# Attention and a top-1 expert layer on one core: the product of the last group of tokens put ahead of the work of the group before it, and the routing of the last four groups put later

## The chip, the cores and the metric

One core of one Trainium2 chip. The metric is the time of one execution on the device in microseconds (us); lower is better.

## What the reference computes

`x` is 64 x 64 tokens of 128 numbers, `ctx` is 64 x 64 tokens of 64 numbers; all data are float32.

```python
def xattn(query, key, value):            # 64 sequences, 64 queries, 64 keys each
    q, k, v = query @ Wq + bq, key @ Wk + bk, value @ Wv + bv
    return softmax(q @ k.T) @ v
def ffn(h):                              # h: 4096 tokens x 128; 8 experts, 512 hidden
    route = sigmoid(h @ Wr + br)
    e = argmax(route, axis=1)            # one expert for each token
    return max(route) * (gelu(h @ W1[e]) @ W2[e])
x = x + tanh(g_xattn) * xattn(layernorm(x), ctx, ctx)
x = x + tanh(g_ffn) * ffn(layernorm(x))
```

## The kernel before

Each engine has an instruction list that is written out by hand, and the engines meet at semaphores. SP issues plain loads, GpSimd (POOL) issues DMAs whose rows go to computed addresses, TensorE (PE) multiplies, ScalarE (ACT) does exp, tanh, gelu and copies, VectorE (DVE) does the rest. An engine that waits blocks everything behind it in its own list.

**Attention part.** The 4096 tokens are 32 tiles of 128, in 8 groups `g` of 4 tiles. Loop `k` runs over the groups on PE, ACT and DVE. In PE's list `scores(k)` forms the products of queries and keys, DVE takes `row_maxima(k)`, ACT takes `exp_scores(k)`, PE does `transpose_probs(k)`, ACT copies it (`copy_probsT`), and PE does `attend(k)`, the product with the values (L1398, 16 matmuls), whose last matmul increments `attn_done`. `project(k + 1)` makes the next queries once DVE's `route_x(k)` has read their bank. DVE's block of `k + 1` begins with `sums(k)`, which waits for `attn_done`, and adds `residual(k, t)`.

**Routing.** `scale_logits(g)`, `bias_logits(g)`, ACT's `tanh_logits(g)` and DVE's `choose(g, 0..6)` choose each token's expert. PE's `prefix(g)` counts the tokens ahead of it, and `place_of_group(g)` and `place_rows(g)` (L762) give the row of the DRAM tensor `scratch` that the token goes to. Each expert has a region there.

**POOL.** In the loop over `at` (L504) POOL writes one tile of 128 token rows a time to `scratch` (L484, 32 times). Before the first tile of a group it waits until that group is placed. `RSTD2_AT` says behind which of the 32 writes the variance of which later group is raised to -1/2 (`rstd2`, L480, a computation and not a DMA). `scatter_tile(j)` (L499) writes finished expert tiles to the output: 4 of them ahead of the writes of group 7 (`EARLY_RESULTS`), the other 32 behind all of them.

**Expert part.** The experts' rows are cut into 25 full tiles `j` of 128 rows and 11 pairs of half tiles. They are laid out in stages as more groups have been placed: `STAGES` holds for each stage how many groups must have been counted and up to which tile it goes. DVE's chain `copy_counts` ... `place_tiles` ... `take_tiles` writes the table of a stage, and SP loads its tiles (L361) when the table is there and the rows of its groups have been written. For each tile ACT normalises the rows (`normalise_tile`, L603) and copies its expert's first weights (L542), PE transposes it (`transpose_tile`, L1445), DVE copies that to SBUF (`copy_transposed`, L1038), PE multiplies (`up`, L1489), ACT takes gelu (L611), PE multiplies (`down`, L1501) and DVE adds (`residual2`, L1043). In PE's loop over `j` the order is `down(j)`, `transpose_tile(j + 3)`, `up(j + 2)`. DVE's loop over `j` is `residual2(j)`, `copy_transposed(j + 3)`, and then the pieces of routing and tables put at this `j`.

Waits are written as `wait_ge(semaphore, count)`; `after(engine, semaphore, g)` waits until step `g` has been done.

Of the kernel before, what the change touches and what calls it, by code (L numbers as in the profile page):

```python
# [14 lines left out]
GT = 4  # L15
# [17 lines left out]
def attention_moe(nc, x, ctx_in, g_xattn, g_ffn, Wq, bq, Wk, bk, Wv, bv, Wr, br, W1, W2, out):  # L33
# [21 lines left out]
    STAGES = [(NG - 5, 5), (NG - 4, 9), (NG - 3, 13), (NG - 1, 21), (NG, FULL), (NG, FULL + HALVES)]  # L55
# [4 lines left out]
    BATCHES = [(0, 0, 5), (1, 5, 4), (2, 9, 4), (3, 13, 4), (3, 17, 4),  # L60
# [8 lines left out]
    RSTD2_AT = {0: 1, 3: 2, 5: 3, 8: 4, 11: 5, 17: 6, 23: 7}  # L69

    RSTD1_AT = 3

    EARLY_RESULTS = 4
# [16 lines left out]
    with ExitStack() as stack:  # L90
# [6 lines left out]
        def bank(name, n=1):  # L97
# [113 lines left out]
        bank_x, bank_q, bank_s, bank_p = (bank("bank_x")[:, 0, :], bank("bank_q")[:, 0, :],  # L211
                                          bank("bank_s")[:, 0, :], bank("bank_p")[:, 0, :])
# [9 lines left out]
        pf_ps = [b[:, GT * S:GT * (S + E)].rearrange("p (t e) -> p t e", t=GT) for b in (bank_p, bank_s)]  # L222
        cnt_ps = [b[:, c:c + E] for b, c in ((banks_o[:, 0, :], 2 * VW), (banks_o[:, 0, :], 2 * VW + E),
                                             (banks_o[:, 0, :], 2 * VW + 2 * E),
                                             (bank_s, GT * (S + E)), (bank_s, GT * (S + E) + E))]
# [80 lines left out]
        def prefix_ps(g):  # L306
            return pf_ps[0 if g < NG - 3 else 1]
# [93 lines left out]
        def _(pool):  # L401
# [102 lines left out]
            for at in range(NG * GT):  # L504
                g, t = divmod(at, GT)
                if at == (NG - 1) * GT:
                    for j in range(EARLY_RESULTS):
                        scatter_tile(j)
                if t == 0:
                    pool.wait_ge(rstd2_ready, g + 1)  # L510
                    pool.wait_ge(placed, g + 1)
                scatter_rows(g, t)

                if at in RSTD2_AT:
                    rstd2(RSTD2_AT[at])
                if at == RSTD1_AT:
                    rstd1(NG - 1)
            for j in range(EARLY_RESULTS, FFN_TILES):
                scatter_tile(j)

        @block.scalar
        def _(act):
# [105 lines left out]
            for k in range(NG):  # L628
# [6 lines left out]
                else:  # L635
# [4 lines left out]
                    copy_v(k)  # L640
                    if k >= NG - 2:
                        tanh_logits(k - 2)
                if k > 0:
                    copy_probsT(k)
                if live(k + 1):
                    copy_qT(k + 1)
# [13 lines left out]
            normalise_tile(2)  # L660
            for j in range(FFN_TILES):
# [6 lines left out]
                if j == 1:  # L668
                    tanh_logits(NG - 2)
                if j == 6:  # L670
                    tanh_logits(NG - 1)

        @block.vector
        def _(dve):
# [102 lines left out]
            def sums(g):  # L777
                dve.wait_ge(attn_done, g + 1)
                nc.vector.reciprocal(inv_sum[:], o_ps[:, :, :, XW:VW]).then_inc(sums_done, 1)

            def residual(g, t):
                at = g * GT + t
                return nc.vector.scalar_tensor_tensor(  # L783
                    out=rows[:, at, 0:XW], in0=o_ps[:, t % 2, t // 2, 0:XW], scalar=inv_sum[:, t % 2, t // 2, :],
# [280 lines left out]
            for k in range(NG):  # L1065
# [59 lines left out]
                c, last = k - 2, k == NG - 1  # L1125
# [5 lines left out]
                if k == 3 or last:  # L1131
                    row_maxima(k)
                if last:
                    place_tiles(0)
                    place_of_group(k - 3)
# [3 lines left out]
                if k == NG - 2:  # L1139
                    copy_counts(0)  # L1140
                if last:
                    scale_logits(c)
                residual(k - 1, 1)
                if k > 3 and not last:
                    row_maxima(k)
                if k == NG - 2:
                    count_tiles(0)
                if last:
                    bias_logits(c)
                if k > 3 and not last:  # L1150
                    place_of_group(k - 3)
                residual(k - 1, 2)
                if k == NG - 2:
                    count_left(0)
                if k > 3:
                    place_rows(k - 3)
                if not last:
                    scale_logits(c)
                if k == NG - 2:
                    sum_tiles(0)  # L1160
                if last:
                    copy_counts(1)
                residual_last(k - 1)
                if last:
                    cap_ends(0)
                else:
                    bias_logits(c)
                if live(k + 1):
                    std1(k + 1)
                if k == 3:  # L1170
                    stats1_of(7, 2, GT)
                if k == NG - 2:
                    pass_experts(0)
                stats2_of(k - 1, 0)
                if last:
                    take_now(0)
                stats2_of(k - 1, 1)
                if k == NG - 2:
                    move_rows(0)
                if last:  # L1180
                    take_tiles(0)
# [6 lines left out]
                if not last:  # L1188
                    aggregate2(k - 1, 2)
                choose(c, 2)  # L1190
                if last:
                    count_tiles(1)
                    aggregate2(k - 1, 2)
                aggregate2(k - 1, 3)
                if last:
                    count_left(1)
                choose(c, 3)
                if last:
                    sum_tiles(1)
                    copy_transposed(0)  # L1200
                    sums(NG - 1)
# [5 lines left out]

            sums_ready(NG - 1)
            residual(NG - 1, 0)
            choose(NG - 3, 5)  # L1210
            residual(NG - 1, 1)
            copy_transposed(1)
            choose(NG - 3, 6)
            residual(NG - 1, 2)
            pass_experts(1)
            copy_counts(2)
            residual_last(NG - 1)
            move_rows(1)
            copy_transposed(2)
            place_tiles(1)  # L1220
            place_of_group(NG - 3)
            scale_logits(NG - 2)
            place_rows(NG - 3)
            bias_logits(NG - 2)
            stats2_of(NG - 1, 0)
            cap_ends(1)
            for j in range(FFN_TILES):
                residual2(j)
                copy_transposed(j + 3)
                if j == 0:  # L1230
                    stats2_of(NG - 1, 1)
                    take_now(1)
                    stats2_of(NG - 1, 2)
                    take_tiles(1)
                    stats2_of(NG - 1, 3)
                    count_tiles(2)
                if j == 1:
                    choose(NG - 2, 0)
                    aggregate2(NG - 1, 0)
                    aggregate2(NG - 1, 1)  # L1240
                    choose(NG - 2, 1)
                    count_left(2)
                    aggregate2(NG - 1, 2)
                    choose(NG - 2, 2)
                    sum_tiles(2)
                    aggregate2(NG - 1, 3)
                    choose(NG - 2, 3)
                    pass_experts(2)
                if j == 2:
                    choose(NG - 2, 4)  # L1250
                    variance2(NG - 1)
                    move_rows(2)
                    choose(NG - 2, 5)
                    place_tiles(2)
                    choose(NG - 2, 6)
                if j == 3:
                    cap_ends(2)
                    take_now(2)
                    take_tiles(2)
                if j == 4:  # L1260
                    place_of_group(NG - 2)
                    place_rows(NG - 2)
                    copy_counts(3)
                    count_tiles(3)
                if j == 5:
                    count_left(3)
                    sum_tiles(3)
                    scale_logits(NG - 1)
                    pass_experts(3)
                    bias_logits(NG - 1)  # L1270
                if j == 6:
                    move_rows(3)
                    place_tiles(3)
                if j == 7:
                    choose(NG - 1, 0)
                    cap_ends(3)
                    choose(NG - 1, 1)
                    take_now(3)
                    choose(NG - 1, 2)
                    take_tiles(3)  # L1280
                    choose(NG - 1, 3)
                if j == 8:
# [343 lines left out]
```

## Time and profile before

| | |
|---|---|
| median of 3 runs | 168.71 us (167.82 to 169.48) |
| the profiled execution, whole | 168.29 us |
| its span, first to last instruction | 166.4 us |
| mean granted TensorE clock | 0.918 of full speed |
| busy: PE, DVE, ACT, POOL | 130.5, 86.6, 88.5, 93.4 us |

The whole execution is its span and 1.9 us around it. A row names line, engine, operation and the tiles it writes and reads (`out<-in`); times are counted from the start of the span. L12 is line 12 of the kernel before.

### The profile page before, as it was taken

The page shows a single profiled execution, that of the slowest core. Times are in us where ns is not written, and L with a number is a line of the kernel's source. Part 1 is how long each engine was busy: PE and PEld are TensorE (multiplying, and loading weights), DVE is VectorE, ACT ScalarE, POOL GpSimd, SP SyncE. Part 2 cuts the span into 40 slices and gives each one's busy share as a digit, 9 for nine tenths or more (in the row PEclk, how much of TensorE's full clock was granted, in tenths as well). Part 3 has the DMA queues.
Part 4 walks back from the last instruction along what each step waited for, and adds up shares of the span by engine and source line. Part 5 has one row for each costly group of instructions (what it writes and reads, how often), then busy time and mean ns, then how long its engine had stood idle before and what let it go on. Part 6 is the DMA issues. An engine that isn't in the chain of part 4 may idle for free.

```text
span 166.4 us, 4830 instructions
## 1 busy us (share of the span) xinstructions
PE 130.5 (78%) x1510; PEld 112.1 (67%) x1511; DVE 86.6 (52%) x533; ACT 88.5 (53%) x206; POOL 93.4 (56%) x143
## 2 busy tenths in 40 slices
PE   6999999999987089799408994041999999898990
PEld 2777777756663089699308993041998989897890
DVE  3699998888898085564205344003822244344230
ACT  2567768687549046397006770033576757485520
POOL 6568877958867574426750067771344444533444
PEclk9999999999999858999965999555799999999999
DMA  4899999401014203112131102310037456460000
GB/s 119 212 274 300 372 312 291 129 18 53 33 36 100 81 16 98 53 37 64 48 95 40 48 33 62 103 63 16 16 102 196 133 135 185 109 174 25 12 22 24
DMA packets 24948, 17.62 MB, mean 106 GB/s; under 512 B 6791, under 2 KB 21835, under 8 KB 24923
## 3 DMA queue, kind: packets, MB, share of 16 engines
q1 hardware_dynamic: 22514, 13.01, 29.4%
q0 software_dynamic: 2176, 4.27, 7.7%
q8 instruction: 13, 0.21, 0.6%
q14 instruction: 13, 0.10, 0.2%
q10 hardware_dynamic: 232, 0.04, 0.1%
HBM read 12.50 MB, written 5.03 MB: 105 GB/s over the span
## 4 chain that ended last, share of the span: by engine, by line
PE 56%; another core or an unknown queue 15%; DVE 14%; issue 9%; ACT 3%; POOL 2%; DVEq 0%; ACTq 0%; POOLq 0%
PE banks_o L1501 12%; PE banks_v L1489 5%; PE bank_q L1489 5%; PE banks_o L1473 4%; PE banks_v L1462 3%; PE bank_s L1321 3%; PE banks_o L1398 2%; PE bank_q L1354 2%; PE bank_p L1489 2%; PE bank_s L1363 2%; PE bank_x L1337 2%; PE bank_x L1445 2%; DVE rows L783 2%; POOL out_dram L499 2%
## 5 line engine op out<-in xcount | busy, mean ns | idle before, releaser
L484 POOL DMA_INDIRECT scratch<-rows,row_at x32 | 31.5, 983 | 26.5 <-DVE row_at L762 19.1
L1043 DVE SCALAR_TENSOR_TENSOR tok<-banks_o,tok 128x128 f32<-128x128 f32 (+1 forms) x36 | 12.6, 350 | 59.5 <-remote 21.8
L1501 PE MATMUL banks_o<-w_sb,hT 128*128 x200 | 29.9, 297 | 12.4 <-issue 6.5
L1501 PEld LDWEIGHTS banks_o<-w_sb,hT 128*128 128x128 f32 x200 | 26.9, 209 | 13.2 <-issue 13.1
L499 POOL DMA_INDIRECT out_dram<-tok x25 | 24.6, 984 | 19.8 <-DVE tok L1043 13.1
L603 ACT ACTIVATE tokn<-tok 128x128 f32<-128x128 f32 (+1 forms) x36 | 17.4, 486 | 8.4 <-remote 4.1
L542 ACT COPY w_now<-w_sb 128x512 f32 x36 | 21.8, 605 | 0.0
L611 ACT ACTIVATE hT<-banks_v 128x512 f32<-128x512 f32 x18 | 10.7, 597 | 18.5 <-remote 8.7
L499 POOL DMA_INDIRECT out_dram<-tok,token_at x11 | 10.9, 989 | 13.4 <-DVE tok L1043 9.5
L1445 PE MATMUL bank_x<-ident,tokn 128*128 128x128 f32 x25 | 7.6, 306 | 13.3 <-DVE toknT L1038 10.7
L611 ACT ACTIVATE hT<-bank_q 128x512 f32<-128x512 f32 x9 | 5.4, 597 | 17.1 <-remote 10.6
L1489 PE MATMUL banks_v<-toknT,w_now 128*128 128x128 f32 x96 | 14.1, 295 | 0.0
L1445 PEld LDWEIGHTS bank_x<-ident,tokn 128*128 128x128 f32 x25 | 3.8, 152 | 14.7 <-issue 14.7
L1473 PE MATMUL banks_o<-w_sb,hT 128*64 x88 | 12.0, 276 | 1.7 <-issue 1.6
L1489 PEld LDWEIGHTS banks_v<-toknT,w_now 128*128 128x128 f32 x96 | 13.1, 212 | 0.0
L1038 DVE COPY toknT<-bank_x 128x128 f32<-128x128 f32 (+1 forms) x36 | 10.1, 280 | 5.6 <-remote 4.6
L586 ACT ACTIVATE probs<-bank_s,minus_max 128x64 f32<-128x64 f32 x32 | 7.4, 315 | 9.4 <-DVE minus_max L745 9.4
L480 POOL TENSOR_TENSOR rows<-rows,minus_half 128x4 f32<-128x4 f32 x8 | 8.3, 1041 | 6.1 <-DVE rows L850 5.7
L1473 PEld LDWEIGHTS banks_o<-w_sb,hT 128*64 128x64 f32 x88 | 9.4, 137 | 2.7 <-issue 2.6
L783 DVE SCALAR_TENSOR_TENSOR rows<-banks_o,inv_sum,x_all 128x136 f32<-128x136 f32 x32 | 10.8, 348 | 0.2
L1476 PE MATMUL banks_o<-w_second,hT 128*64 128x128 f32 x80 | 10.8, 276 | 0.0
L435 POOL TENSOR_TENSOR mv<-mv,minus_half 128x4 f32<-128x4 f32 x8 | 8.1, 1014 | 4.4 <-DVE mv L691 4.4
(205 smaller groups left out, 323.0 us busy)
## 6 DMA issues: line engine op xcount, KB each, us to landing
w_second<-in_L_ffn_W_dram SPq DMA_DIRECT2D x10, 256.0 KB, 2.8
w_sb<-in_L_ffn_W_dram SPq DMA_DIRECT2D x1, 2048.0 KB
x_all<-in_x_dram SPq DMA_DIRECT2D x7, 256.0 KB, 4.1
tok<-scratch SPq DMA_DIRECT2D x25, 66.0 KB, 1.9
ctx<-in_ctx_dram SPq DMA_DIRECT2D x8, 128.0 KB, 3.8
tok<-scratch SPq DMA_DIRECT2D x21, 33.0 KB
scratch<-pad_rows SPq DMA_DIRECT2D x1, 528.0 KB
scratch<-rows,row_at POOLq DMA_INDIRECT x32
```

What stands on the lines that cost most here:

```text
L484: nc.gpsimd.indirect_dma_start(out=scratch, out_offset=bass.IndirectOffsetOnAxis(ap=row_at[:, g * GT + t:g * GT + t + 1], axis=0), in_=row ...
L499: nc.gpsimd.indirect_dma_start(out=out_tok, out_offset=bass.IndirectOffsetOnAxis(ap=at, axis=0), in_=tok[j][0:n, 0:D], in_offset=None, bou ...
L542: nc.scalar.copy(w1_now[j % DEEP][:], w1_sb[:, bass.ds(w_at[j], F)]).then_inc(w1_copied, 1)
L603: nc.scalar.activation(tokn[j % 2][0:n, :], tok[j][0:n, 0:D], ACT.Identity, bias=tok[j][0:n, SHIFT:RSTD], scale=tok[j][0:n, RSTD:SCALE]).t ...
L611: nc.scalar.activation(hT[j % DEEP][:], h_ps[j % DEEP], ACT.Gelu).then_inc(gelu_done, 1)
L783: return nc.vector.scalar_tensor_tensor(out=rows[:, at, 0:XW], in0=o_ps[:, t % 2, t // 2, 0:XW], scalar=inv_sum[:, t % 2, t // 2, :], in1= ...
L1043: nc.vector.scalar_tensor_tensor(out=tok[j][0:n, 0:D], in0=y_ps[j % 2][0:n, :], scalar=tok[j][0:n, SCALE:TOKEN], in1=tok[j][0:n, 0:D], op0 ...
L1445: nc.tensor.transpose(tT_ps, tokn[j % 2][:], ident[:]).then_inc(toknT_done, 1)
L1473: last = nc.tensor.matmul(y_ps[j % 2][0:H, :], hT[j % DEEP][:, c * P:c * P + H], w2_sb[:, bass.ds(w_at[j] + c * D, D)], start=(c == 0), st ...
L1476: last = nc.tensor.matmul(y_ps[j % 2][H:P, :], hT[j % DEEP][:, c * P + H:c * P + P], w2_second[p][:, c * D:(c + 1) * D], start=(c == 0), s ...
L1489: last = nc.tensor.matmul(h_ps[j % DEEP][:, c * P:(c + 1) * P], w1_now[j % DEEP][:, c * P:(c + 1) * P], toknT[j % DEEP][:], start=True, st ...
L1501: last = nc.tensor.matmul(y_ps[j % 2], hT[j % DEEP][:, c * P:(c + 1) * P], w2_sb[:, bass.ds(w_at[j] + c * D, D)], start=(c == 0), stop=(c ...
```

## The change

Five things are altered together.

- PE's last two groups are written out: `scores(7)` goes ahead of `attend(6)`, `project_values(7)` behind it. `project(7)` goes ahead of `prefix(3)`. The product of group 7 goes to another pair of banks (`last_o_ps`), so that it no longer waits for DVE to have read the product of group 6.
- On ACT `copy_qT(7)` goes ahead of `copy_v(6)`, and `copy_v(7)` behind `copy_probsT(7)`.
- The choices of groups 4 to 7 and their placing go later on DVE. Group 4 is placed in block `j = 2` of the expert loop, and no longer in `k = 7`; group 5 in `j = 5` (before: ahead of the loop), group 6 in `j = 8` (before: 4), group 7 in `j = 10` as before.
- Stage 3 counts 6 groups and goes to tile 17 (before: 7 groups, tile 21).
- POOL's `rstd2(4)`, `rstd2(5)` and `rstd2(7)` move among the 32 writes (from behind writes 8, 11 and 23 to behind 11, 15 and 21), and no output is written ahead of the writes of group 7.

```diff
-    STAGES = [(NG - 5, 5), (NG - 4, 9), (NG - 3, 13), (NG - 1, 21), (NG, FULL), (NG, FULL + HALVES)]
+    STAGES = [(NG - 5, 5), (NG - 4, 9), (NG - 3, 13), (NG - 2, 17), (NG, FULL), (NG, FULL + HALVES)]
-    RSTD2_AT = {0: 1, 3: 2, 5: 3, 8: 4, 11: 5, 17: 6, 23: 7}
+    RSTD2_AT = {0: 1, 3: 2, 5: 3, 11: 4, 15: 5, 17: 6, 21: 7}
-    EARLY_RESULTS = 4
...
+        last_o_ps = banks_sp[:, :, 0:2 * VW].rearrange("p b (t c) -> p b t c", c=VW)
...
-                if at == (NG - 1) * GT:
-                    for j in range(EARLY_RESULTS):
-                        scatter_tile(j)
...
# DVE, attention part
+                if k == NG - 2:
+                    sums(k - 1)
+                    choose(3, 5)
+                    route_x(k)
+                    sums_ready(k - 1)
+                    residual(k - 1, 0)
+                    choose(3, 6)
+                    row_maxima(k)
+                    copy_counts(0)
+                    residual(k - 1, 1)
+                    count_tiles(0)
+                    place_of_group(3)
+                    residual(k - 1, 2)
+                    count_left(0)
+                    place_rows(3)
...
+                if k == NG - 1:
+                    row_maxima(k)
+                    take_now(0)
...
+                    sums(k - 1)
+                    variance2(k - 2)
...
+            sums(NG - 1)
+            pass_experts(1)
             sums_ready(NG - 1)
+            copy_transposed(0)
             residual(NG - 1, 0)
...
# DVE, expert loop (steps 2 to 6 of group 4's choice at j = 0, group 5's at 2 to 4,
# group 6's at 6 and 7, group 7's at 8)
+                if j == 2:
+                    place_of_group(4)
+                    aggregate2(7, 0)
+                    aggregate2(7, 1)
+                    place_rows(4)
...
+                if j == 5:
+                    place_of_group(5)
+                    place_rows(5)
...
+                if j == 8:
+                    place_of_group(6)
                     take_now(3)
+                    choose(7, 0)
+                    place_rows(6)
...
# PE
             def attend(g):
...
-                after(pe, x2_ready, g - 1)
+                if g < NG - 1:
+                    after(pe, x2_ready, g - 1)
...
+            before_last, last_group = NG - 2, NG - 1
+            scores(before_last)
+            project(last_group)
+            prefix(before_last - 3)
+            project_values(before_last)
+            transpose_probs(before_last)
+            scores(last_group)
+            count_groups(1, before_last)
+            attend(before_last)
+            project_values(last_group)
+            transpose_probs(last_group)
+            transpose_route(last_group)
+            keep_busy(2, bank_x)
+            attend(last_group)
...
+                if j == 1:
+                    prefix(4)
+                    count_groups(2)
+                if j == 4:
...
+                    prefix(5)
+                    count_groups(3)
+                if j == 7:
...
+                    prefix(6)
```

## Rows read from the trace of the kernel before

**Rows 1.** The waits between 36 and 125 us: waiter, releaser, total us, times, longest

```profile
ACT hT L611 <- remote: 21.9, 3, 8.7
```

**Rows 2.** PE's instructions in order: `attend(7)`, then the transpose of tile 0

```profile
51.60 0.70 PE L1398 MATMUL banks_o<-values,probsT 64*64 64x137 f32 x16
...
53.50 0.33 PE L1445 MATMUL bank_x<-ident,tokn 128*128 128x128 f32 x1
```

**Rows 3.** DVE in the same stretch: the two instructions that waited for these

```profile
58.33 0.29 DVE L1038 COPY toknT<-bank_x 128x128 f32<-128x128 f32 x1 [4.23 <-remote]
58.54 0.17 DVE L779 RECIPROCAL inv_sum<-banks_o 128x4 f32<-128x4 f32 x1
```

**Rows 4.** POOL in order: first and last DMA of runs of 6, 4, 8 (first only), 13

```profile
49.58 1.03 POOL L484 DMA_INDIRECT scratch<-rows,row_at  x1 [0.20 <-POOL rows L480]
...
55.96 0.95 POOL L484 DMA_INDIRECT scratch<-rows,row_at  x1 [0.30 <-issue]
...
64.30 0.95 POOL L484 DMA_INDIRECT scratch<-rows,row_at  x1 [1.91 <-DVE row_at L762]
...
68.09 0.96 POOL L484 DMA_INDIRECT scratch<-rows,row_at  x1 [0.31 <-issue]
...
75.91 1.03 POOL L484 DMA_INDIRECT scratch<-rows,row_at  x1 [3.79 <-DVE row_at L762]
...
96.47 0.96 POOL L484 DMA_INDIRECT scratch<-rows,row_at  x1 [10.57 <-DVE row_at L762]
...
111.85 0.98 POOL L499 DMA_INDIRECT out_dram<-tok  x1 [0.31 <-issue]
```

**Rows 5.** PE in order: `down(j)` for j = 2, 4, 7, 10, 12, 13, 17

```profile
67.22 1.06 PE L1501 MATMUL banks_o<-w_sb,hT 128*128 x8
...
73.08 1.14 PE L1501 MATMUL banks_o<-w_sb,hT 128*128 x8
...
78.84 1.06 PE L1501 MATMUL banks_o<-w_sb,hT 128*128 x8
...
93.64 1.14 PE L1501 MATMUL banks_o<-w_sb,hT 128*128 x8
...
97.51 1.06 PE L1501 MATMUL banks_o<-w_sb,hT 128*128 x8
...
99.41 1.06 PE L1501 MATMUL banks_o<-w_sb,hT 128*128 x8
...
121.86 1.06 PE L1501 MATMUL banks_o<-w_sb,hT 128*128 x8
```

**Rows 6.** POOL in order: write 6, and `rstd2(4)`, which the change moves

```profile
38.54 1.03 POOL L484 DMA_INDIRECT scratch<-rows,row_at  x1 [0.19 <-issue]
...
42.38 1.04 POOL L480 TENSOR_TENSOR rows<-rows,minus_half 128x4 f32<-128x4 f32 x1 [0.27 <-issue]
```

**Rows 7.** All engines in order: `attend(5)`, `sums(5)` that waited for it, `project(7)`

```profile
41.63 0.70 PE L1398 MATMUL banks_o<-values,probsT 64*64 64x137 f32 x16 [0.24 <-ACT probsT L580]
...
43.07 0.18 DVE L779 RECIPROCAL inv_sum<-banks_o 128x4 f32<-128x4 f32 x1 [0.68 <-PE banks_o L1398]
...
44.42 1.02 PE L1354 MATMUL bank_q<-xnT,wqk_sb 128*128 128x512 f32 x2
```

**Rows 8.** DVE in order: `residual2(1)`

```profile
67.19 0.35 DVE L1043 SCALAR_TENSOR_TENSOR tok<-banks_o,tok 128x128 f32<-128x128 f32 x1 [1.32 <-PE banks_o L1501]
```

**Rows 9.** Stretches: busy us of PE, PEld, DVE, ACT, POOL; clock; DMA, GB/s

```profile
40.00:50.00 10.00, 8.91 (x114) 6.34 (x115) 9.18 (x72) 6.04 (x21) 7.31 (x8) 1.00 0.13 42
...
57.00:58.00 1.00, 0.00 (x0) 0.00 (x0) 0.00 (x0) 0.00 (x0) 0.00 (x0) 0.53 0.20 68
...
63.00:64.00 1.00, 1.00 (x7) 1.00 (x7) 0.82 (x7) 1.00 (x3) 0.00 (x0) 0.56 0.13 42
```

**Rows 10.** DVE in order: `residual2(4)`, in whose block group 6 was placed

```profile
74.25 0.35 DVE L1043 SCALAR_TENSOR_TENSOR tok<-banks_o,tok 128x128 f32<-128x128 f32 x1 [1.17 <-PE banks_o L1501]
```

**Rows 11.** The page's DMA issues: the loads of full tiles, median us to landing

```profile
tok<-scratch SPq DMA_DIRECT2D x25, 66.0 KB, 1.9
```

More of the change, by code:

```diff
@@ L517, in _ @@
                     rstd1(NG - 1)
-            for j in range(EARLY_RESULTS, FFN_TILES):
+            for j in range(FFN_TILES):
                 scatter_tile(j)
@@ L1123, in _ @@
                     continue
-                c, last = k - 2, k == NG - 1
+                if k == NG - 2:
+                    sums(k - 1)
[12 more added lines that the diff above has]
+                    place_rows(3)
+                    sum_tiles(0)
+                    residual_last(k - 1)
+                    std1(k + 1)
+                    pass_experts(0)
+                    stats2_of(k - 1, 0)
+                    move_rows(0)
+                    stats2_of(k - 1, 1)
+                    place_tiles(0)
+                    stats2_of(k - 1, 2)
+                    cap_ends(0)
+                    continue
+                if k == NG - 1:
+                    row_maxima(k)
+                    take_now(0)
+                    stats2_of(k - 2, 3)
+                    take_tiles(0)
+                    aggregate2(k - 2, 0)
+                    aggregate2(k - 2, 1)
+                    aggregate2(k - 2, 2)
+                    aggregate2(k - 2, 3)
+                    sums(k - 1)
+                    variance2(k - 2)
+                    dve.wait_ge(sums_done, k)
+                    residual(k - 1, 0)
+                    residual(k - 1, 1)
+                    scale_logits(4)
+                    route_x(k)
+                    residual(k - 1, 2)
+                    bias_logits(4)
+                    residual_last(k - 1)
+                    copy_counts(1)
+                    stats2_of(k - 1, 0)
+                    count_tiles(1)
+                    stats2_of(k - 1, 1)
+                    count_left(1)
+                    stats2_of(k - 1, 2)
+                    sum_tiles(1)
+                    stats2_of(k - 1, 3)
+                    continue
+                c = k - 2
                 sums(k - 1)
@@ L1130, in _ @@
                 sums_ready(k - 1)
-                if k == 3 or last:
+                if k == 3:
                     row_maxima(k)
-                if last:
-                    place_tiles(0)
-                    place_of_group(k - 3)
                 residual(k - 1, 0)
@@ L1380, in transpose_probs @@
                 after(pe, probsT_copied, g - 1)
-                after(pe, place_done, 0 if g == 2 else g - 3)
+                after(pe, place_done, 0 if g == 2 else min(g - 3, 3))
                 for p in range(GT // 2):
@@ L1529, in _ @@
             pe.wait_ge(consts_ready, 1)
-            for k in range(NG):
+            for k in range(NG - 2):
                 scores(k)
```

245 lines of the change are left out of this document (107 added, 138 removed).

## The prediction, made before the changed kernel was run

> **What bounds the kernel now.** I read first the busy time by stretches, then the waits, then each engine's instructions in order. The kernel has two parts. Up to about 53 us DVE sets the pace of the attention loop: it is busy 9.18 of the 10 us from 40 to 50 [rows 9]. From then on PE should set it: `down` of tile 12 and of tile 13 lie 1.9 us apart [rows 5], which is the pace of a full tile. The expert part does not keep it. ACT's gelu alone waited 21.9 us in three waits whose releaser the view does not name [rows 1]. Reading the engines side by side shows what they have in common: PE has finished, and the engine that waits for it starts much later. `attend(7)` was over at 52.3 us and the transpose of tile 0 at 53.8, but DVE used them at 58.54 and 58.33 [rows 2, 3]. In the meantime nothing ran but POOL, which issued indirect DMAs one straight behind another, a start every 1.3 us. I call that a run. The one that covers this stall has 6 DMAs, and DVE goes on 2.3 us after the last one's start [rows 3, 4]. Three later runs, of 4, 8 and 13 DMAs, each lie over a stall of the tile loop [rows 4, 5]. So my reading is: a completion of PE that falls some 2.5 us or more behind the start of a run is mostly held until about 2.3 us behind the start of its last DMA.
>
> The price of a run, by its length: of 6, 58.33 - 53.83 = 4.5 us. Of 4, two tiles took 73.08 - 67.22 = 5.9 instead of 3.8 us, so 2.1. Of 8, three tiles took 93.64 - 78.84 = 14.8 instead of 5.7, so 9.1. Of 13, four tiles took 121.86 - 99.41 = 22.45 instead of 7.6, so 14.85 [rows 5]. Together 30.5 of 168.3 us. Two or three DMAs alone cost little: `attend(5)` ended at 42.33, behind three writes, and DVE had it at 43.07 [rows 6, 7].
>
> The Trainium skill, in "SBUF — State Buffer", section "SBUF: two separate sides", says that only VectorE and GpSimd contend for a port and that "PE, ACT, and DVE's dedicated pair never wait on anyone". By that rule POOL's DMAs hold nothing of PE; it is weighed as rival B's companion below.
>
> **The change, part by part**, against the profiled execution of 168.29 us (the median of the runs is 0.4 us above it).
>
> 1. *`rstd2(4)` moves from behind write 8 to behind write 11.* It costs POOL the same 1.04 us, but it now splits the writes elsewhere. Before, writes 6 to 8 are followed by it at 42.38 [rows 6]. Now 6 to 11 follow each other from 38.54: a run of 6, its last start at 38.54 + 5 x 1.28 = 44.95, so PE's completions are free at 47.2. `attend(5)` ends at 42.33, 3.8 us into the run, where in the earlier run of 6 one at 2.7 us was held to the end. DVE's whole block of `k = 6` stands behind `sums(5)`. It started at 43.07, it would start at 47.2: +4.1 us. Bounds: 0 (released as before) and 4.1. I take 4.1, by the equal run.
>
> 2. *Less in DVE's block of `k = 6`, `scores(7)` earlier.* 15 instructions leave the block (the logits and choice of group 4, the aggregates), 4 come in (`place_tiles(0)`, `cap_ends(0)`). 72 instructions, the large ones among them, took 9.18 us [rows 9]; I take 0.1 for a small one. That is 1.1 us by which the row maxima of group 7 come earlier, and with them exp, `attend(7)` and tile 0. Bounds 0 and 1.3. -1.1 us. Table 0 is ready earlier too, but the tiles' landing was not the last wait.
>
> 3. *`project(7)` ahead of `prefix(3)`.* `project(7)` takes 1.02 us and waits for `route_x(6)` [rows 7]; DVE's `place_of_group(3)` now waits for both, and POOL for it. Bounds 0 and 1.3; +0.5 us.
>
> 4. *Group 4 placed in the expert loop.* Ahead of the loop POOL now has only the 4 writes of group 3. The run of 6 that cost 4.5 becomes one of 4 at 2.1: -2.4 us.
>
> 5. *The clock.* In that stall the granted clock fell to 1.2 GHz at 57.5 and rose to 2.4 GHz at 63.6 [rows 9], with PE at work from 58.8. 4.8 us of work at half speed are 2.4 at full: -2.4 us if the gap ahead of tile 0 stays short. Bounds 0 and -2.4; with a run of 4 the gap is 2 us, and it took 3.7 us of idle PE for the fall, so I take all.
>
> 6. *The runs of the expert loop.* Before 4, 8 and 13. After: writes 18 to 21 (4), group 6 (4, since no output goes with it), then group 7 and all outputs finished by then. Group 7 is placed in block 10 as before, and by the time of the hold outputs 0 to 12 were finished before as well (4 early, 9 in the run of 13), so 4 + 13 = 17. A DMA more is 1.29 us, so 14.85 + 4 x 1.29 = 20.0. Sum 2.1 + 2.1 + 20.0 = 24.2 instead of 26.05: -1.8 us. Bounds -4 and +4 (three outputs fewer or more in the run). So the early outputs were no loss: the same DMAs are only put elsewhere.
>
> 7. *Tile 9 later.* Stage 2 needs the writes of group 4. From `residual2` to the first write of a group placed in its block take 75.91 - 74.25 = 1.7 us [rows 4, 10], then the four writes and `rstd2(6)` 5.1 to the last start, 2.3 until it is through, 1.9 for the load [rows 11], 0.5 to normalise: 11.5 us. PE wants tile 9 four tiles, 7.6 us, later. 3.9 us late, of which 2.1 are the run of 4 in item 6: +1.8. Bounds 0 and 3.9.
>
> 8. *At nothing.* The choices put into blocks 0 to 8 are up to 14 instructions a block, 1.3 us at 0.1 each, beside the two fixed ones, under the 1.9 us of a tile; if PE stopped covering them they would cost 0.5. The smaller stage 3 and larger stage 4 load in stretches where the table and the writes come 2 tiles or more ahead. `copy_v(7)` behind `copy_probsT(7)`: 0.3, within item 2. The other banks for group 7 take a wait away, for `residual(6, 3)`, that was over before `attend(7)` was due.
>
> Sum: 4.1 - 1.1 + 0.5 - 2.4 - 2.4 - 1.8 + 1.8 = -1.3, so 167.0 us.
>
> **The rivals.**
>
> *A, the forecast*: the sum above. Its own range, from the bounds of items 5 to 7, is 164.5 to 170.
>
> *B, the run in the attention loop holds nothing that matters.* For it: in runs of 4 or more single completions slipped through. DVE had tile 1's product at 67.19, in the middle of the run of 4 [rows 4, 8], and the attention loop's completions come thick. Then item 1 is 0 and 168.3 - 5.4 = 162.9; if the run of group 3 is then over ahead of `attend(7)`, too, up to 2 less: 162 us. By the skill's rule no run holds anything; the stalls would have another cause, and the likeliest result of that is rival D.
>
> *C, slower: the hold lets the clock fall inside the attention loop.* PE has nothing to do from about 43.5 (the end of `attend(5)` at 42.33 and some 1.2 us of scores) to 47.5 (`project(7)` behind `route_x(6)`), 4.0 us; a gap of 3.7 was enough at 57.5 [rows 9]. [...] Then project, values, transposes and scores of groups 6 and 7, about 3.5 us of PE work, take 3.5 more, partly beside DVE; `prefix(3)` is later, and with it the run of group 3, so that it lies over `scores(7)` and holds the row maxima for another 2 us. 167.0 + 4.4 = 171.4 us. Against it: keeping only part of the hold avoids it all.
>
> *D, the stalls belong to the tiles and not to POOL.* The stall ahead of tile 0 and those at tiles 2, 7 and 13 stay, and only items 2 and 7 act: 169 us. Against it: four of four stalls end about 2 to 3 us behind a run's last start.
>
> **How the numbers follow.** A 0.42, B 0.28, C 0.18, D 0.08, else 0.04. 1% is 1.7 us, about what a measurement of this kernel can tell from no change, so faster is below 167.0 and slower above 170.4. A lies astride that bound: of its 0.42, 0.22 fall below, 0.16 within, 0.04 above. B gives 0.28 faster, C 0.02 within and 0.16 slower, D 0.07 within and 0.01 faster, the rest 0.04 slower or within. Faster 0.51, same 0.26, slower 0.23. The range is from B's 161.5 to C's 171.8. For the median of the runs the point is the same within 0.4 us; I keep 167.0.
>
> **What the profile of the changed kernel would show.** Item 1: POOL writes 6 to 11 without a gap over 0.3 us, and `sums(5)` on DVE near 47 us (A, C) or near 43 (B). Item 4: no stall of over 3 us between the transpose of tile 0 and its copy. Item 5: the clock at 1.0 while tiles 0 to 2 are multiplied; for C, the clock at 0.5 within 47 to 55 us. Item 6: one run of about 17 DMAs behind write 28, with PE stopped for some 20 us, and no stall at tile 7 of more than 3 us. Item 7: the normalising of tile 9 waiting for its load. The prediction would be wrong if long runs are not what holds PE's completions, if the last run grows well past 17, or if the loop meets a run at a point where one completion more or less is enough to shift a whole group.

## The result, and the profile after

The changed kernel takes 176.98 us (median of 4 runs, 176.23 to 177.69), the kernel before 168.59 beside it: ratio 1.050, 95% interval 1.042 to 1.057. It is slower, where 167.0 was forecast. Executions of one kernel fall into a faster and a slower kind; the ratios and their intervals compare the faster ones alone, and the times given are medians of all. The profiled execution spans 174.4 us (before 166.4) at a mean granted clock of 0.881 (before 0.918).

In the rows, `<-issue` stands behind idle time in which the engine waited for nothing that the profile shows, and `<-remote` behind idle time that nothing in the profile ended. `down(j)` in PE's order, j = 2, 4, 5, 6, 14; then the transpose of tile 17 and `down(15)`:

```profile
68.75 1.15 PE L1546 MATMUL banks_o<-w_sb,hT 128*128 x8 [0.19 <-issue]
...
72.64 1.06 PE L1546 MATMUL banks_o<-w_sb,hT 128*128 x8
75.44 1.15 PE L1546 MATMUL banks_o<-w_sb,hT 128*128 x8
77.44 1.06 PE L1546 MATMUL banks_o<-w_sb,hT 128*128 x8
...
104.14 1.15 PE L1546 MATMUL banks_o<-w_sb,hT 128*128 x8 [2.39 <-issue]
116.65 0.45 PE L1490 MATMUL bank_x<-ident,tokn 128*128 128x128 f32 x1 [11.36 <-issue]
124.05 2.07 PE L1546 MATMUL banks_o<-w_sb,hT 128*128 x8 [5.23 <-ACT hT L612]
```

Against [rows 5], with `down(13)` at 99.69 and `down(17)` at 130.58:

| stretch | before | after | difference | forecast |
|---|---|---|---|---|
| start to `down(2)` | 67.22 | 68.75 | +1.5 | -1.3 |
| `down(2)` to `down(13)` | 32.2 | 30.9 | -1.3 | -5.2 |
| `down(13)` to `down(17)` | 22.45 | 30.9 | +8.4 | +5.15 |
| `down(17)` to the end | 44.5 | 43.8 | -0.7 | 0 |

The attention part, all engines in order:

```profile
42.03 0.70 PE L1443 MATMUL banks_o<-values,probsT 64*64 64x137 f32 x16 [0.24 <-ACT probsT L581]
...
45.33 0.96 POOL L488 DMA_INDIRECT scratch<-rows,row_at  x1 [0.30 <-issue]
...
47.64 0.18 DVE L786 RECIPROCAL inv_sum<-banks_o 128x4 f32<-128x4 f32 x1 [4.86 <-remote]
48.16 2.04 PE L1398 MATMUL bank_q<-xnT,wqk_sb 128*128 128x512 f32 x2 [3.13 <-DVE x_all L759]
...
53.91 1.19 PE L1443 MATMUL banks_o<-values,probsT 64*64 64x137 f32 x16
...
57.82 0.18 DVE L786 RECIPROCAL inv_sum<-banks_o 128x4 f32<-128x4 f32 x1 [1.98 <-remote]
...
61.78 0.29 DVE L1045 COPY toknT<-bank_x 128x128 f32<-128x128 f32 x1 [0.41 <-PE bank_x L1490]
```

`attend(5)` is over at 42.73, and DVE uses it at 47.64, 2.3 us behind the start of the sixth DMA in a row [rows 7 of before: 43.07]. PE then waits 3.13 us for DVE, and `project(7)` takes 2.04 us in place of 1.02. The clock says why (stretches: PE, PEld, DVE, ACT, POOL busy; clock; DMA share, GB/s):

```profile
40.00:50.00 10.00, 5.76 (x47) 2.83 (x46) 4.17 (x30) 4.02 (x14) 5.84 (x6) 0.88 0.12 41
50.00:60.00 10.00, 9.67 (x81) 7.80 (x80) 6.19 (x43) 4.53 (x10) 4.95 (x5) 0.50 0.27 63
...
100.00:110.00 10.00, 2.91 (x24) 2.53 (x22) 0.96 (x8) 1.60 (x3) 7.69 (x8) 0.79 0.25 75
110.00:120.00 10.00, 2.17 (x9) 1.91 (x9) 2.46 (x11) 0.00 (x0) 7.56 (x9) 0.50 0.27 80
120.00:130.00 10.00, 5.95 (x29) 5.96 (x30) 2.51 (x13) 4.35 (x9) 2.42 (x3) 0.52 0.15 44
```

From 50 to 60 PE is at work at half speed, 1.2 GHz. The profiles of e5, e13 and e16, which are the same kernel, show this again: DVE uses `attend(5)` at 46.5 to 46.9, and the clock is 0.50 from 50 to 60. And from 100 to 120 PE is busy for 5 us of 20, while POOL issues one long run, 18 DMAs of which these are the first and last (before: 13 [rows 4]):

```profile
97.66 0.95 POOL L488 DMA_INDIRECT scratch<-rows,row_at  x1 [2.68 <-DVE row_at L769]
...
119.47 0.98 POOL L503 DMA_INDIRECT out_dram<-tok  x1 [0.30 <-issue]
```

One wait is new, ACT's for the rows of a tile, 6.7 us in two times, with PE behind it at tile 9 and then `down(8)`:

```profile
81.14 0.49 ACT L604 ACTIVATE tokn<-tok 128x128 f32<-128x128 f32 x1 [4.68 <-DMA tok<-scratch]
81.69 0.39 PE L1490 MATMUL bank_x<-ident,tokn 128*128 128x128 f32 x1 [3.19 <-ACT tokn L604]
...
87.36 1.15 PE L1546 MATMUL banks_o<-w_sb,hT 128*128 x8 [0.78 <-ACT hT L612]
```

### The profile page after: what moved, and what is told of

Its sections match the earlier page's. It is cut to its first block, busy times and chain, and to the rows that moved or that the text cites. A ratio compares the mean times of both kernels' runs of the same rounds, so it can differ in the third digit from the quotient of the medians.

```text
span 174.4 us, 4819 instructions
## 1 busy us (share of the span) xinstructions
PE 135.0 (77%) x1505; PEld 114.9 (66%) x1506; DVE 86.4 (50%) x533; ACT 88.4 (51%) x206; POOL 93.1 (53%) x143
## 4 chain that ended last, share of the span: by engine, by line
PE 58%; issue 16%; another core or an unknown queue 12%; DVE 5%; SPq 3%; DMA 2%; POOL 2%; ACT 1%; DVEq 0%; POOLq 0%; ACTq 0%
PE banks_o L1546 10%; PE banks_v L1418 5%; PE bank_q L1398 4%; PE banks_o L1518 4%; PE banks_v L1534 4%; PE bank_q L1534 3%; PE banks_o L1443 3%; PE banks_sp L1365 3%; PE banks_v L1507 3%; PE banks_sp L1407 3%; DMA tok<-scratch 2%; PE bank_x L1381 2%; POOL out_dram L503 2%; PE banks_sp L1534 2%
## 5 line engine op out<-in xcount | busy, mean ns | idle before, releaser
L1050 DVE SCALAR_TENSOR_TENSOR tok<-banks_o,tok 128x128 f32<-128x128 f32 (+1 forms) x36 | 12.6, 349 | 59.1 <-remote 22.7
L503 POOL DMA_INDIRECT out_dram<-tok,token_at x11 | 10.7, 976 | 13.3 <-DVE tok L1050 11.6
L587 ACT ACTIVATE probs<-banks_sp,minus_max 128x64 f32<-128x64 f32 x32 | 7.4, 314 | 13.0 <-DVE minus_max L752 13.0
L612 ACT ACTIVATE hT<-banks_sp 128x512 f32<-128x512 f32 x8 | 4.7, 589 | 18.1 <-remote 17.9
L1534 PE MATMUL banks_v<-toknT,w_now 128*128 128x128 f32 x96 | 13.6, 288 | 0.0
L1518 PE MATMUL banks_o<-w_sb,hT 128*64 x88 | 11.9, 275 | 1.3 <-issue 1.2
L1534 PEld LDWEIGHTS banks_v<-toknT,w_now 128*128 128x128 f32 x96 | 12.6, 204 | 0.0
L1398 PE MATMUL bank_q<-xnT,wqk_sb 128*128 128x512 f32 x16 | 9.4, 669 | 3.5 <-DVE x_all L759 3.1
L1418 PE MATMUL banks_v<-wvg_sb,ctxT 65*128 65x137 f32 x64 | 11.0, 324 | 0.0
```

Of the source, the lines that this page charges most:

```text
L503: nc.gpsimd.indirect_dma_start(out=out_tok, out_offset=bass.IndirectOffsetOnAxis(ap=at, axis=0), in_=tok[j][0:n, 0:D], in_offset=None, bou ...
L612: nc.scalar.activation(hT[j % DEEP][:], h_ps[j % DEEP], ACT.Gelu).then_inc(gelu_done, 1)
L1050: nc.vector.scalar_tensor_tensor(out=tok[j][0:n, 0:D], in0=y_ps[j % 2][0:n, :], scalar=tok[j][0:n, SCALE:TOKEN], in1=tok[j][0:n, 0:D], op0 ...
L1398: nc.tensor.matmul(bank_q[0:QR, :], wqk_sb[:], xnT[g % 2][:], start=True, stop=True).then_inc(qT_done, 1)
L1418: last = nc.tensor.matmul(v_ps[:, p, b, :], ctxT[g % 3][:, p, b, :, :].rearrange("c t k -> c (t k)"), wvg_sb[:], start=True, stop=True)
L1518: last = nc.tensor.matmul(y_ps[j % 2][0:H, :], hT[j % DEEP][:, c * P:c * P + H], w2_sb[:, bass.ds(w_at[j] + c * D, D)], start=(c == 0), st ...
```

## The experiments

They ran on five chips, a group of them on each, always beside the kernel before. That turned out to be the first finding. On two chips the kernel before takes 133.5 us (e1 to e4) and 133.4 us (e9 to e12); on three it takes 168.4 (e5 to e8), 168.0 (e13 to e15) and 167.5 us (e16 to e18), as in the first measurement. I call the first kind free and the second kind held. Each chip was used on one occasion only, so the runs don't part the chip from the occasion. The theories at the start: **T1**, a run of back-to-back DMAs of POOL holds PE; **T2**, the stalls belong to tiles or loads; **T3**, any work of POOL holds PE; **T4** (later called A), the new order of the attention part costs. From the second group on: **S**, the rows of groups 4 and 7 come too late.

### e1 to e4, on a free chip

```diff
e1  -    RSTD2_AT = {0: 1, 3: 2, 5: 3, 11: 4, 15: 5, 17: 6, 21: 7}      (changed kernel)
    +    RSTD2_AT = {0: 1, 3: 2, 5: 3, 8: 4, 15: 5, 17: 6, 21: 7}
e2  +                if at == 6 * GT:                                    (changed kernel)
    +                    for j in range(EARLY_RESULTS):                  # 4
    +                        scatter_tile(j)
e3  +    nc.gpsimd.tensor_tensor(pause_out[:, n, :]..., pause_in[:]..., minus_half[:]..., ALU.pow)
    # behind every second of the first 20 outputs                        (changed kernel)
e4  -    EARLY_RESULTS = 4                                               (kernel before)
    +    EARLY_RESULTS = 0
```

> The changed kernel with POOL's rstd2(4) back behind write 8, so that writes 6 to 11 are 3 + 3 again; all else is as changed. T1 (a long unbroken run of POOL's indirect DMAs holds TensorE's completions): DVE has attend(5) near 43.5 us and not at 47.9, the clock is not at 0.5 between 50 and 60, and tile 0's transpose comes 4 to 5 us earlier than at 61.3; of these up to 3 us may be given back where the loop meets the next run at another tile, so 172 to 174 us. T4 (the new order of TensorE and ScalarE costs, and not the run): DVE still waits until after 46 us, and the time stays at 177. T2 (the stalls belong to tiles or loads): 176 to 177.

> The changed kernel with 4 outputs put behind the writes of group 5 again (a run of 8 there), so that the last run has 14 DMAs and not 18. T1: the last run's excess over four tiles falls from 23.3 us by 4 or 5 DMAs at 1.3 us, to 17 to 18 us; the run of 8 in the middle costs up to 5 us more than the one of 4, so 173 to 177 us, with the loss moved from tile 14 to tile 8 or 9. T2 (the stalls belong to tiles or loads): tile 14 stalls 20 us as in the changed kernel and the time is 177 us.

> The changed kernel with a POOL computation of some 1.04 us (a power, on tiles of its own that nobody reads) after every second of the first 20 outputs; POOL has 10 us more work. T1: the last run is broken into runs of 2, TensorE's completions come through between them, tiles 14 to 17 no longer stall for 20 us: 160 to 168 us. If the computation must be longer than 1 us to let completions through: 177 us. T3 (any work of POOL holds them): the stall grows with POOL's work, 180 to 185 us. T2: 177 us.

> The kernel before with no output ahead of the writes of group 7, the one part of the change that makes its run of 8 a run of 4 and its run of 13 one of 17 or 18. T1: the stall at tile 7 falls from 9.1 to some 2 to 5 us, that of the last run grows from 14.9 to 20 to 23 us; together 167 to 172 us. T4 (the order in the attention part is what costs): 168.5 us, no difference. T2: 168.5 us.

Beside 133.5 us: e1 146.6 (ratio 1.091, 1.081 to 1.101), e2 147.2 (1.105, 1.098 to 1.111), e3 152.3 (1.134, 1.123 to 1.144), e4 133.8 (1.003, 0.997 to 1.009). No number of mine fits: none of the stops is there. In e4, whose last run of DMAs is unbroken from 78.46 to 124 us, the windows show PE at work beside it without a gap:

```profile
80.00:100.00 20.00, 20.00 (x177) 19.72 (x177) 10.88 (x57) 15.07 (x31) 15.43 (x16) 1.00 0.49 135
```

POOL's DMAs are the same on both kinds of chip (983 ns a write in the page of before, 985 in e4's). So whether T1 acts is not decided by the kernel but by where it runs. Yet e1 and e2, near kin of the changed kernel, lose 10% here too, and for another reason. Their waits name it: ACT for the rows of a tile, 11.6 us in e1 and 12.1 us in e2. e3 is slower than e2 by 5.1 us, by the medians. In e9, the same kernel on the other free chip, the stretch behind `down(24)` is 4.8 us longer than in e2, and POOL's DMAs follow one another to the end with 0.3 us between them: its list, with 11.3 us more in it (104.6 against 93.3 us busy), sets the time there.

### e5 to e8, on a held chip

e5 is the changed kernel. The others are the kernel before with POOL's times of the change in the expert part, and nothing else of it. `rstd2(4)` and `rstd2(5)` stay where they were in all three, so that none of them has item 1's run of 6:

```diff
e6, e8  -    STAGES = [..., (NG - 1, 21), ...]      BATCHES: (3, 17, 4)
        +    STAGES = [..., (NG - 2, 17), ...]      BATCHES: (4, 17, 4)
e7, e8  +                if t == 0 and g in WRITES_BEHIND:
        +                    pool.wait_ge(y_added, WRITES_BEHIND[g])
e7      WRITES_BEHIND = {4: 4}, rstd2(6) behind write 15
e8      WRITES_BEHIND = {4: 4, 5: 6, 6: 10, 7: 11}, rstd2(6), rstd2(7) behind 15 and 21,
        EARLY_RESULTS = 0
```

> The changed kernel itself, beside the kernel before on this chip. H (the chip decides whether completions of TensorE are held under POOL's runs; the four kernels e1 to e4 ran where they are not, the kernel before in 133.5 us there): 169 and 177 us where they are held, 133.5 and 145 to 149 us where they are not. Not H (the held completions came from something in the kernels e1 to e4 that differs from the changed one): 177 us, with the kernel before at 133.5 us.

> The kernel before with the change's stages alone: stage 3 counts 6 groups and ends at tile 17, so that tiles 17 to 20 belong to the stage that needs the rows of group 7. S (late rows and not the order of the attention part are the cost): where nothing is held, tile 17's rows come some 2.5 us after TensorE wants them and the clock falls once, so 3 to 7 us above the kernel before; where completions are held, within 3 us of it. A (the order in the attention part costs): no difference.

> The kernel before with POOL's writes of group 4 held back until tile 3 is finished (as late as the change's placing in block 2 has them), and rstd2(6) behind write 15 in place of 17; all else as before. S: tile 9's rows come 2 to 4 us late, with a fall of the clock in the gap: 4 to 8 us above the kernel before where nothing is held. A: no difference.

> The kernel before with all of the change's times for POOL: its stages, its writes of group 4 behind tile 3, 5 behind 5, 6 behind 9 and 7 behind 10, rstd2(6) and rstd2(7) behind writes 15 and 21, no output ahead of the writes of group 7; the attention part, DVE's blocks, ACT and the order on TensorE as before. S: as slow as the changed kernel within 2 us where nothing is held (145 to 149), and where completions are held 172 to 179 us. A: as fast as the kernel before within 3 us.

Beside 168.35 us: e5 176.8 (1.061, 1.047 to 1.076; the medians give 1.050), e6 167.7 (0.997, 0.989 to 1.006), e7 174.4 (four runs of 171.4 to 175.4, without an interval: 6.1 above by the medians, 5.6 by the lowest of each), e8 172.4 (1.029, 1.016 to 1.042). H of e5 stands, its opposite falls. The stages alone cost nothing here: PE is stopped by the last run when tile 17 is due. Late writes of group 4 alone cost about 6 us, but not in the way of my item 7. They put the writes of groups 4 and 5 into a run of 8 (70.0 to 78.9), and `down(6)` to `down(7)` takes 10.0 us, from 74.91 to 84.95. The changed kernel has no such run, since `rstd2(6)` and `rstd2(7)` break its writes from 71.60 to 83.10 into 2, 4 and 2. e8 costs 4.0 of the 8.4 us that e5 does, by the medians. The other 4.4 lie in what e8 leaves out: the run of 6 from item 1, DVE's blocks and the order of the attention part. No run on a held chip parts them, and e1, which was made to undo the run of 6, met a free one.

### e9 to e12, on the second free chip

e9 is e3 again and e12 is e8 again. e10 and e11 are the kernel before with an instruction of POOL put between DMAs: e10 the power of e3 behind every second one from write 13 to output 11 (unless an `rstd2` stands there), e11 a memset of one number per partition behind every one from write 9 to the last output.

```diff
e10 +                if at > 12 and at % 2 and at not in RSTD2_AT:
    +                    pause(at)                    # power, 1.04 us
    +                if j < 12 and j % 2:             # in scatter_tile(j)
    +                    pause(32 + j)
e11 # pause(n): nc.gpsimd.memset(pause_out[:, n, 0:1], 0.0), behind every DMA
```

> The changed kernel with a POOL computation of some 1.04 us after every second of the first 20 outputs, once more, for a chip where completions of TensorE are held (the kernel before at 168 us there). T1 (an unbroken run of indirect DMAs holds them): down of tiles 13 to 17 no longer takes 30 us but under 18, and the time falls from 177 to 160 to 168. T3 (any POOL work holds them): the stall grows, 180 us or more. T2 (tiles or loads): 177 us. Where the kernel before takes 133.5 us nothing is held, and this kernel takes 152 us as before.

> The kernel before with the same POOL computation behind every second DMA from write 13 on, up to output 11, where no rstd2 stands already, so that no run has over 2 or 3 DMAs; nothing else differs. T1: where completions are held, the stalls of 4.5, 2.1, 9.1 and 14.9 us go and 20 us or more are won, 140 to 150 us. T3: slower than before by up to 10 us. T2: 168 us. Where nothing is held: 134 to 137 us, since POOL has 10 us more work.

> The kernel before with a POOL memset of one number per partition behind every DMA from write 9 on and behind every output. If the hold is broken by any other instruction of POOL between two DMAs: 140 to 150 us where completions are held. If it is broken only by the time that passes without a DMA being made (a memset is short): 165 to 170 us. Where nothing is held: 133 to 136 us.

> The kernel before with all of the change's times for POOL (its stages, the writes of group 4 behind tile 3, 5 behind 5, 6 behind 9, 7 behind 10, no early outputs), the attention part and the lists of the other engines as before, for a chip where nothing is held. S (the rows of groups 4 and 7 come late for tiles 9 and 17): 144 to 149 us there, with the kernel before at 133.5. A (the order in the attention part costs): 133 to 136 us. Where completions are held: 172 us as before.

Beside 133.4 us: e9 151.3 (1.134, 1.128 to 1.139), e10 139.8 (1.050, 1.045 to 1.055), e11 134.1 (1.003, 0.999 to 1.007), e12 146.5 (1.101, 1.095 to 1.106). e10's 139.8 is above the 134 to 137 that I expected there. e12 decides for S on free chips: the kernel before, with its own attention part and POOL's times of the change in the expert part alone, loses 13.1 us, as much as e1 and e2 (13.1 and 13.7), each of which has all of the change but one piece. The changed kernel itself never ran on a free chip. ACT's list in e12 shows the two places, tiles 9 and 17:

```profile
72.21 0.49 ACT L607 ACTIVATE tokn<-tok 128x128 f32<-128x128 f32 x1 [5.52 <-DMA tok<-scratch]
...
93.83 0.49 ACT L607 ACTIVATE tokn<-tok 128x128 f32<-128x128 f32 x1 [6.18 <-DMA tok<-scratch]
```

and its stretches that each gap brings the clock down for the tiles behind it:

```profile
70.00:75.00 5.00, 2.24 (x11) 2.25 (x12) 1.76 (x13) 2.53 (x7) 3.95 (x4) 0.73 0.44 95
...
90.00:95.00 5.00, 0.63 (x3) 0.63 (x4) 1.26 (x7) 1.17 (x3) 3.78 (x5) 0.78 0.34 89
95.00:100.00 5.00, 5.00 (x27) 5.00 (x26) 1.94 (x11) 2.70 (x6) 3.78 (x5) 0.54 0.43 112
```

Against e4, `down(6)` to `down(9)` takes 11.2 instead of 5.7 us and `down(14)` to `down(17)` 13.0 instead of 5.9: 12.6 us, and the spans differ by 144.1 - 132.2 = 11.9.

### e13 to e15, on the second held chip

The changed kernel, e10 and e11 once more.

> The changed kernel itself once more. Where nothing is held (the kernel before at 133.5 us): as e12 by theory S, 145 to 149 us. Where completions are held (the kernel before at 168 us): 177 us, as twice before.

> The kernel before with a POOL computation of 1.04 us behind every second DMA (e10). T1 (an unbroken run of DMAs holds TensorE's completions): where they are held, 140 to 150 us in place of 168. T3 (any POOL work holds them): 170 us or more. T2 (the stalls belong to tiles or loads): 168 us. Where nothing is held: 139.8 us as measured.

> The kernel before with a POOL memset of one number per partition behind every DMA (e11). If any other instruction between two DMAs lets completions through: 140 to 150 us where they are held. If only time without a DMA being made does: 165 to 170 us. Where nothing is held: 134 us as measured.

Beside 168.0 us: e13 177.3 (1.053, 1.044 to 1.061), e14 157.5 (0.934, 0.925 to 0.942), e15 169.6 (1.011, 1.006 to 1.015). POOL is busy for 15.6 us more in e14 (109.0 against 93.4) and the kernel is 10.5 us shorter: T3 and T2 fall, and T1 holds here, short of its forecast (140 to 150). The memset of e15 does nothing, and its rows show that it takes no time either: it fits into the 0.3 us that lie between two DMAs anyway, and they start 1.26 us apart as ever.

```profile
98.35 0.95 POOL L489 DMA_INDIRECT scratch<-rows,row_at  x1 [0.19 <-issue]
99.30 0.11 POOL L486 MEMSET pause_out<- 128x1 f32 x1
99.61 0.96 POOL L489 DMA_INDIRECT scratch<-rows,row_at  x1 [0.19 <-issue]
```

What is left in e14 is the clearest picture of a stop. The profile is of its longest execution, 158.5 us. Its last pause is at 106.87; from 108.11 to 122.30 POOL issues 12 DMAs without one. In that stretch PE crawls, a matmul at a time, where a group of eight, with no wait inside it, is one row of 1.06 us in [rows 5]:

```profile
117.02 0.27 PE L1472 MATMUL banks_v<-toknT,w_second 128*64 128x64 f32 x1 [1.07 <-issue]
119.22 0.37 PE L1511 MATMUL banks_o<-w_sb,hT 128*128 x1 [1.93 <-issue]
119.95 0.37 PE L1511 MATMUL banks_o<-w_sb,hT 128*128 x1 [0.37 <-issue]
121.48 0.57 PE L1511 MATMUL banks_o<-w_sb,hT 128*128 x1 [1.15 <-issue]
123.59 0.37 PE L1511 MATMUL banks_o<-w_sb,hT 128*128 x1 [1.55 <-issue]
```

So not only PE's completions come late, as I had put it: PE doesn't get on with its own list either. e18 below shows single matmuls with such gaps too, of 0.3 to 0.6 us, from 123 to 131 us.

### e16 to e18, on the third held chip

e16 is the changed kernel. e17 is e14 with the pauses up to output 33; e18 has one behind every third DMA from write 14 on.

```diff
e17 -                if j < 12 and j % 2:
    +                if j < 34 and j % 2:
e18 +                if at in (14, 20, 26, 28, 31):
    +                if j in (1, 6, 9, 12, 15, 18, 21, 24, 27, 30, 33):
```

> The changed kernel itself. Where nothing is held (the kernel before at 133.5 us), theory S: 146 to 148 us, as the kernel before with the change's times for POOL (e12, 146.5). If the order in the attention part adds to that, over 149. Where it is held: 177 us.

> e14 with the pauses behind every second output to the end (11 more, and POOL 11 us more work). T1: where completions are held, down of tile 24 is followed by the half tiles without a stop of 15 us, and the time falls from 157.5 to 147 to 153 us, where POOL's own work ends it. If the stop at 111 to 126 us in e14 had another cause, the half tiles with their second weights: 157 to 165 us. Where nothing is held: 145 to 150 us, POOL's work.

> The kernel before with a pause behind every third DMA from write 12 on, to the end. If a run of 3 holds no more than a run of 2 does: 145 to 150 us where completions are held, since POOL has less to do than in e17. If the hold begins with the third DMA: 155 to 165 us. Where nothing is held: 138 to 143 us.

Beside 167.5 us: e16 174.8 (1.048, 1.037 to 1.059), e17 153.2 (0.919, 0.912 to 0.926), e18 155.8 (0.938, 0.929 to 0.947). e17 is the fastest version here, 14.3 us under the kernel before, though POOL is busy for 122.5 us in place of 93.4; 153.2 lies just above what I expected (147 to 153), and 19.8 us above the free chips' 133.4. The stretches 80 to 100 and 100 to 120 us of e17, and after them those of the kernel before:

```profile
80.00:100.00 20.00, 18.74 (x162) 18.00 (x160) 10.84 (x61) 14.37 (x30) 17.28 (x18) 1.00 0.32 85
100.00:120.00 20.00, 18.04 (x250) 16.53 (x250) 6.11 (x22) 11.71 (x24) 17.23 (x17) 1.00 0.61 168
```

```profile
80.00:100.00 20.00, 13.13 (x107) 12.96 (x108) 6.78 (x41) 8.81 (x18) 7.56 (x8) 0.83 0.20 55
100.00:120.00 20.00, 8.07 (x49) 7.46 (x48) 6.55 (x37) 4.57 (x9) 11.68 (x12) 0.66 0.18 54
```

PE is busy 36.8 of the 40 us in place of 21.2, beside more of POOL's work, and the clock doesn't fall. At the end of e17 POOL is the bound: its DMAs and pauses follow each other to 148.8 us. Runs of three cost 2.7 us more than runs of two by the medians, with 9 pauses fewer, so the third DMA in a row seems to hold something. What the pause does is open: the computation of e17 also moves the DMAs apart in time, the memset of e15 doesn't, and no run spaces them out without a computation. On free chips pauses are a loss (e10, +5%), so that neither version is the better one everywhere.

## Why the prediction was wrong

The forecast was 10.0 us short by the medians. In the profiles 9.3 us are missing: 2.8 up to `down(2)`, 3.9 from there to `down(13)`, 3.3 to `down(17)`, and 0.7 the other way behind it.

**The step that failed up to `down(2)` is the sum of items 1 to 4: it takes the hold of 4.1 us and puts the clock's fall inside the attention part at nothing.** That fall was left to rival C, with a chance of 0.18. Item 1 itself was right: `sums(5)` came at 47.64 (forecast 47.2). But PE was nearly idle from 43.6 to 48.2 us, the clock fell, and it stayed at 1.2 GHz from 50 to 60 us while PE, now setting the pace, worked through groups 6 and 7. C's mechanism came with it. C placed the following hold over `scores(7)`; it was `attend(6)`, which ended under the four writes of group 3 (51.89 to 55.76), with DVE at 57.82. The copy of tile 0 came at 61.78 instead of 58.33 [rows 3]: +3.4, where items 1 to 4 make +1.1. From `sums(5)` to that copy 14.1 us passed where the items leave 12.3, and 0.4 us were lost ahead of `attend(5)` already. **Item 5** came nearly true: no run lies ahead of tile 0 any more (0.41 us of wait, not 4.23), the clock was back at 1.0 from 62 us on, and the stretch from the copy to `down(2)` took 1.9 us less, of the 2.4 forecast. What the item overlooked is that the gap which pulls the clock down had moved into the attention part. Its reading of the gap was a little off too: the 0.53 over 57 to 58 us in [rows 9] means that the clock was down for nearly all of that microsecond, 3.2 us and not 3.7 behind PE's last matmul. Nor did any item price that the change leaves 2 of the 7 fillers `keep_busy` that PE ran at the end of the attention part; no run tests them. That this part of the loss comes from item 1's run is read from the profile and not shown by a run of its own.

**Item 6 was right in its mechanism and mis-sized.** The last run had 18 DMAs, not 17, and held tiles 13 to 17 for 30.9 - 7.6 = 23.3 us, not 20.0. One more DMA explains 1.3 of the 3.3 us. It began 2.0 us ahead of `down(13)` in place of 2.9, which is 0.9. And from the start of its last DMA to `down(17)` 11.1 us passed in place of 10.0, which is 1.1: `down(15)`, `up(17)` and `down(16)` ran at the lower clock behind the run (2.07, 1.91 and 1.91 us), before it was `down(15)` alone, and in part (1.45). That "the early outputs were no loss" was so in count only. On a free chip they are neutral (e4); on a held one the price of a run isn't linear in its length, and this was not tried by itself.

**Item 7 had the late rows right and left out what they cost besides.** `down(6)` to `down(8)` took 9.9 us, an excess of 6.1 for the 3.9 in the sum. The sum took 2.1 of these for a hold, but no hold shows there: the run of 4 had its first two DMAs ahead of a gap of 0.83 us, ACT waited 4.68 us for the load, and PE 3.19 for ACT. The transpose of tile 9 came 3.4 us late. The rest is what follows a gap: `up(8)` and `down(7)` at the lower clock (1.94 and 1.84 us in place of 1.06 each), and ACT's gelu late by 0.8 for `down(8)`, behind its wait for DVE's logits. That e7 costs 6.1 as well is chance, for it has another run of DMAs (8, not 2, 4 and 2). The other run of 4 does hold: DVE uses `down(10)`, over at 92.6, at 96.01, 2.0 us behind the last start, and `down(12)` is 2.5 us late (forecast 2.1). The rest of the 3.9 us missing between tiles 2 and 13 is spread over small waits, 0.9 of it ahead of `down(5)`.

**Item 8 was wrong**, which the first measurement hides. That "the table and the writes come 2 tiles or more ahead" does not hold for tile 17 once its rows include those of group 7: the last write starts at 101.44, so by my own 2.3 and 1.9 us the rows are there at 105.6, and at 1.9 us a tile the transpose was due behind that of tile 16 (100.59) at 102.5. Here the long run had stopped PE anyway (e6: no cost). On a free chip it is the larger half of the loss (e12: 7.0 of 12.6 us).

**Rival B** fell with item 1. **Rival D** fell on held chips with e14 and e17. That the change would be slower was given 0.23, and its range ended 5 us short, since C's price (4.4), the rest of item 7's bound (2.1) and the upper bound of item 6 (4) were never added to one another; together they reach 177.5. All three came, at least in part.

## What to carry to other kernels

Ask of every step put later which load is the first that needs its rows, and work out its arrival against the pace of the tiles as if all present stalls were gone; a stall can cover a late load and hand it back on another chip. Losses that one change can bring about together may all come, and the range must hold their sum. Wherever an item of the sum leaves TensorE idle, ask what the clock does behind it and price that in the same item. Where an engine stops beside a run of GpSimd DMAs, break the run with a computation of a microsecond and look: two kernels of the same lists, one broken and one not, tell more than any reading of waits.

## What the runs showed of the hardware

- The same kernel takes 133.4 to 133.5 us on two chips and 167.5 to 168.4 us on three. On the latter TensorE stops while GpSimd issues indirect DMAs 1.27 us apart; a computation of 1.07 us behind every second one takes 14.3 us of the time away (e17, 153.2 us), a memset of 0.11 us nothing (e15, 169.6). What differs between the chips, or between the occasions, no run here shows.
- The Trainium skill, in "SBUF — State Buffer", section "SBUF: two separate sides", has TensorE wait for no one. On the free chips the trace agrees (20.00 of 20 us busy beside 16 DMAs in e4); on the held ones TensorE stops all the same (8.07 of 20 beside 12), but no run says that a port of SBUF is the place, so that this doesn't refute the sentence.
- A gap in TensorE's work can cost twice: after 3.9 us without a matmul (e12, 68.8 to 72.8 us) the clock was 0.50 from 73 to 75 us, which is 1.2 GHz, and `down(7)` to `down(8)` took 2.4 instead of 1.9 us; the longer gap at tile 17 left the clock at 0.54 from 95 to 100 us.
